# Ternary MLP with Strassen-type layers: the fourth operand difference of each square layer made by VectorE instead of GpSimd

## The reference

```python
Q, K, V = x @ wq.T, x @ wk.T, x @ wv.T                 # D = 64
energy = einsum('bnd,bne->bde', K, V)
x = layernorm(x + ((Q @ energy) * sqrt(3/64)) @ wo.T)
h = silu(x @ w1.T * s1) * (x @ w2.T * s2)              # 256 -> 1024
h = gelu(h @ h1.T * t1)                                # 1024 -> 1024, weights -1, 0, 1 (times 8)
h = gelu(h @ h2.T * t2)                                # 1024 -> 1024
x = layernorm(x + h @ w3.T * s3)                       # 1024 -> 256
```

## Time and profile before

| | us |
|---|---|
| median of 3 runs | 682.74 |
| lowest, highest | 681.18, 683.98 |
| profiled execution | 685.8 |
| its span on the core | 684.0 |
| TensorE matmuls busy | 652.7 (95%) |
| VectorE busy | 473.7 (69%) |
| ScalarE busy | 396.1 (58%) |
| GpSimd busy | 269.5 (39%) |
| mean granted TensorE clock | 0.984 of full speed |

### The profile page before, as it was taken

The page is one execution under the profiler, slowest core; times in us unless marked ns, Lnnn a source line. Parts: engine busy times, 40 slices in busy tenths (PEclk is TensorE's granted clock), DMA queues, the critical chain, the costliest instruction groups (busy, mean ns, idle before and its releaser), DMA issues.

```text
span 684.0 us, 9189 instructions
## 1 busy us (share of the span) xinstructions
PE 652.7 (95%) x3197; PEld 540.7 (79%) x3198; DVE 473.7 (69%) x718; ACT 396.1 (58%) x669; POOL 269.5 (39%) x214
## 2 busy tenths in 40 slices
PE   8978799989999999999999999999999999999992
PEld 7656587878879888688888888688888888888892
DVE  1365457588655898388856799388856799488467
ACT  1366569856764457465854456565755366656660
POOL 1527699169000366049100267039200267077002
PEclk9999999999999999999999999999999999999997
DMA  8997898934440025633440015633340005444101
GB/s 316 410 402 275 301 353 259 333 150 147 146 143 1 0 54 197 242 124 124 129 173 6 1 27 198 252 139 123 124 156 29 1 12 193 165 152 156 63 1 63
DMA packets 24087, 105.02 MB, mean 154 GB/s; under 512 B 2192, under 2 KB 3280, under 8 KB 16208
## 3 DMA queue, kind: packets, MB, share of 16 engines
q1 hardware_dynamic: 24032, 104.29, 43.3%
HBM read 89.60 MB, written 22.02 MB: 163 GB/s over the span
## 4 chain that ended last, share of the span: by engine, by line
PE 78%; DVE 10%; DMA 7%; issue 3%; ACT 1%; SPq 0%; POOL 0%; POOLq 0%; DVEq 0%; ACTq 0%
PE ps L1139 51%; PE ps L1084 16%; PE ps L1196 7%; DVE R L807 4%; DMA xr<-in_xT 2%; DMA w_dram<-in_w2T 2%; DMA w<-w_dram 1%; DVE xr L791 1%; PE ps L1004 1%; PE ps L988 1%; PE ps L1040 1%; DVE quarter L801 1%; DMA out<-xr 1%; PE ps L1026 1%; DVE st L780 1%
## 5 line engine op out<-in xcount | busy, mean ns | idle before, releaser
L1139 PE MATMUL ps<-R,ring 128*128 128x512 f32 x1792 | 414.1, 392 | 4.7 <-issue 4.7
L1139 PEld LDWEIGHTS ps<-R,ring 128*128 128x128 f32 x1792 | 337.7, 189 | 76.6 <-issue 6.6
L807 DVE TENSOR_TENSOR R<-quarter,R 128x512 fp32r<-128x512 f32 x288 | 255.3, 908 | 89.0 <-ACT R L583 88.7
L583 ACT CAST R<-quarter 128x512 fp32r<-128x512 f32 x288 | 175.3, 615 | 26.5 <-POOL quarter L468 10.0
L1084 PE MATMUL ps<-x1T,w 128*128 128x512 f32 x512 | 122.1, 398 | 4.3 <-DVE x1T L751 3.8
L1084 PEld LDWEIGHTS ps<-x1T,w 128*128 128x128 f32 x512 | 97.7, 192 | 26.9 <-issue 2.7
L629 ACT ACTIVATE quarter<-U,sc 128x512 f32<-128x512 f32 x96 | 69.4, 723 | 74.4 <-DVE U L826 32.1
L421 POOL TENSOR_TENSOR ve<-mv,eps 128x4 f32<-128x4 f32 x14 | 5.4, 388 | 235.6 <-DVE mv L784 235.6
L446 POOL TENSOR_TENSOR quarter<-quarter,quarter 128x512 f32<-128x512 f32 x32 | 49.4, 1544 | 118.8 <-ACT quarter L629 109.7
L549 ACT ACTIVATE sg<-ps,sc 128x512 f32<-128x512 f32 x64 | 44.1, 690 | 72.4 <-PE ps L1084 72.2
L599 ACT COPY U<-ps 128x512 f32<-128x512 f32 x96 | 56.3, 586 | 43.1 <-PE ps L1139 43.0
(11 more groups left out here) (66 smaller groups left out, 325.7 us busy)
## 6 DMA issues: line engine op xcount, KB each, us to landing
ring<-combos SPq DMA_DIRECT2D x56, 1024.0 KB, 4.9
combos<-unit SPq DMA_DIRECT2D x8, 1024.0 KB, 8.5
xr<-in_xT SPq DMA_DIRECT2D x13, 512.0 KB, 6.6
unit<-in_h1T SPq DMA_DIRECT2D x4, 1024.0 KB, 11.7
xr<-in_x_rows SPq DMA_DIRECT2D x8, 512.0 KB, 8.0
unit<-in_h2T SPq DMA_DIRECT2D x4, 1024.0 KB, 9.5
out<-xr SPq DMA_DIRECT2D x7, 512.0 KB, 3.0
w<-w_dram SPq DMA_DIRECT2D x3, 1024.0 KB, 8.2
```

The source lines that it names most:

```text
L583: nc.scalar.copy(R[slot_of(p, u)][:, 0, c, :], quarter[operand_home(p, u)][:, c, :]).then_inc(hi_done, 1)
L807: nc.vector.tensor_tensor(r[:, 1, c, :], quarter[operand_home(p, u)][:, c, :], r[:, 0, c, :].bitcast(f32), ALU.subtract).then_inc(lo_done, 1)
L1139: last = nc.tensor.matmul(ps[:, bank + j, :], w, view(R[slot_of(p, u)][:, part, k, :]), start=n in (0, 1, 5) and k == 0 and part == 0, sto ...
```

## The change

The four chunks of the fourth difference, x21 <- x21 - t2, go from GpSimd's `further_differences` to VectorE, into a new function called behind each `lo` of operand u0+2. They get a semaphore of their own, `t4_done`, since two engines can't share one count; `t_done` counts twelve a layer. ScalarE's cast for operand n = 4 and its gelu 1 (which overwrites t2) wait for the new semaphore as well.

```diff
         def n_t(L, i):
-            return 16 * L + i + 1
+            return 12 * L + i + 1
...
-            return {2: 2 * c + 1, 3: 8 + c, 4: 12 + c, 5: 2 * c}[n]
+            return {2: 2 * c + 1, 3: 8 + c, 5: 2 * c}[n]
...
             def further_differences(p, l):
...
-                for c in range(KH):
-                    pool.wait_ge(lo_done, n_split(p, u0 + 1, c))
-                    nc.gpsimd.tensor_tensor(x21[:, c, :], x21[:, c, :], t2[:, c, :], ALU.subtract).then_inc(t_done, 1)
...
-                elif n in (2, 3, 4, 5):
+                elif n == 4:
+                    act.wait_ge(t4_done, KH * L + c + 1)
+                elif n in (2, 3, 5):
                     act.wait_ge(t_done, n_t(L, t_of(n, c)))
...
-                    act.wait_ge(t_done, n_t(L, 15))
+                    act.wait_ge(t_done, n_t(L, 11))
+                    act.wait_ge(t4_done, KH * (L + 1))
...
+            def fourth_difference(p, l, c):
+
+                L, u0 = 2 * p + l, NPROD * l
+                x21, t2 = quarter[homes(p, l)[1]], quarter[homes(p, l)[4]]
+                dve.wait_ge(lo_done, n_split(p, u0 + 1, c))
+                dve.wait_ge(t_done, n_t(L, 2 * c + 1))
+                nc.vector.tensor_tensor(x21[:, c, :], x21[:, c, :], t2[:, c, :], ALU.subtract).then_inc(t4_done, 1)
...
                 for j in range(KH):
                     lo(p, u0 + 2, j)
+                    fourth_difference(p, l, j)
                 for j in range(KH + 1):
                     if j < KH:
                         add_first(L, j)
```

More of the change, by code:

```diff
@@ L176, in build @@
         l1_tile, silu_done, h_made = sem("l1_tile"), sem("silu_done"), sem("h_made")
-        t_done, hi_done, lo_done = sem("t_done"), sem("hi_done"), sem("lo_done")
+        t_done, t4_done, hi_done, lo_done = sem("t_done"), sem("t4_done"), sem("hi_done"), sem("lo_done")
         prod, cp_done, add_done, gelu_done = sem("prod"), sem("cp_done"), sem("add_done"), sem("gelu_done")
@@ L460, in further_differences @@
                 L, u0 = 2 * p + l, NPROD * l
-                x11, x21, _, _, t2 = (quarter[i] for i in homes(p, l)[:5])
+                x11, t2 = quarter[homes(p, l)[0]], quarter[homes(p, l)[4]]
                 for c in range(KH):
```

## The result

The changed kernel took 698.18 us (median of 6 runs, 695.47 to 702.87) against 683.50 for the kernel before (6 runs): ratio 1.0226, 95% interval 1.0181 to 1.027, or 14.7 us more. It is slower, as forecast; the forecast was 20.3 us more, and 698.18 lies inside the range of 694 to 709, in its lower half. Its profiled execution took 697.44 us with a span of 695.7.

What follows compares the result with a forecast made beforehand. TensorE, busy 95% of the span, was taken to bound the kernel; its waits and clock falls over the eight layers summed to 20.3 us, giving 703.0 us on the median of 682.74, range 694 to 709.

Steps and rivals of the forecast that it cites:

- the first rival: Waits of TensorE come but the clock does not fall: 14.7 us more, so 697.4; chance 0.20.
- What bounds, and that the removal gives TensorE nothing directly: TensorE, busy 95% of the span, bounds; ScalarE's casts waited 10.0 us for GpSimd's subtractions, TensorE never did.
- The price of an added instruction: Each added VectorE subtraction: 0.6 us alone, 1.7 beside GpSimd's 128x512 instructions, the high end nearer.
- Layer 2, step by step: First add 6.9 us later, copy done at 268.7, fourth product waits 2.2; layer costs 2.5, layer 4 the same.
- The two delays: Layer 2: the fourth product's wait and the later xr load are the same 2.25 us, not added.
- Layer 0: GpSimd runs without a break; wait of 4.4 us at the fourth product plus 1.7 for the clock: 6.1.
- Layers 6 and 7: Waits of 2.2 and 2.6 us at the fourth products; with the clock 3.9 and 4.3.
- The fall of the clock after them: Half clock after the waits in layers 6 and 7, costing 1.7 us in each.
- Layers 1, 3 and 5: Add 2.5 to 4.8 us later, copy 0 to 1.0 after its turn; cost 0, 0.5 and 0.5.
- The sum: Over layers 0 to 7: 6.1 + 0 + 2.5 + 0.5 + 2.5 + 0.5 + 3.9 + 4.3 = 20.3 us.

Runs made afterwards that it cites:

- late: Changed kernel with the four subtractions still on VectorE but placed behind the layer's first normalisation: 680.35 us, ratio 0.9950 to the kernel before.
- no_third: Changed kernel with GpSimd's L465 (the third difference) left out, output not that of the reference: 680.77 us, ratio 0.9962 to the kernel before.
- the second profile: The changed kernel run once more, nothing altered, for another profile: 699.43 us (4 runs), ratio 1.0198 to the kernel before.

## Why the prediction was right, and where its sizes were off

The range held and the path was right. The central figure, 703.0, is 4.8 us too high, and the first rival (no fall of the clock, 697.4, given 0.20) is nearer to the measured 698.18. Its 14.7 us equals the measured 14.7, but that is a coincidence: it has no fall in layer 0, where there was one, and about 0.5 us each in layers 3 and 5, where there was nothing.

- **What bounds, and that the removal gives TensorE nothing directly.** Right. TensorE is the only engine whose waits count. What GpSimd's relief is worth goes by way of the normalisation (1.38 us instead of 4.30), which here is behind the late adds; `late` shows it, where nothing delays the adds, as the two waits for xr that go.
- **The price of an added instruction.** Right. 0.60 us alone and 1.70 beside GpSimd, four of eight at each price in layer 2. The step rested on reading the low parts of the kernel before in two places with and without GpSimd, and `no_third` shows that GpSimd is the cause.
- **Layer 2, step by step.** The add was forecast 9.3 us after the first low part and came 9.2 after; the copy 6.1 after the add, measured 6.2; TensorE's delay was 2.2, as forecast. The two delays, of the product and of the load for xr, proved to be one: the second wait stayed at 1.10, where it had been 1.39. Layers 2 and 4 took 2.1 and 2.3 us more; the 2.5 had a fall of the clock in it, and the clock stayed at 1.00.
- **Layer 0.** The wait was right: counted from the layer's start, the fourth product starts 4.3 us later than before in the first profile and 4.7 in the second, against 4.4 forecast. (The idle time in brackets, 3.19 and 4.40, differs by more, since in the first profile layer 0 began with 5.2 us at half clock, in the second with 3.4, and TensorE's own lateness eats into the wait.) That the whole came to 6.0 against 6.1 is partly luck: it holds one stretch of 3.4 us at half clock behind the wait, and the second profile had two there, for 7.6 us.
- **Layers 6 and 7.** The waits were right (2.2 and 2.6 forecast; the fourth products start 2.2 us late in both, and the layers are 2.4 us longer). The fall of the clock after them, 1.7 us each, did not come in either profile. This is the term of the sum that was mis-sized: 3.4 us, and 0.5 in layers 2 and 4 with it. I had put gaps of 2.2 us beside the gap of 1.89 with a fall. But 2.2 was the delay of the next matmul's start, and 1.89 an idle time as the profile brackets it; like against like it was 1.6 against 1.89, nearer to the 1.39 without one. Nor was 1.89 the smallest gap with a fall, as the first rival says: the kernel before has a fall at a gap of 1.50 as well, in the front part (TensorE's row, then its clock). The three gaps that I had picked made the clock look more regular than it is.

```profile
43.70 12.74 PE L1084 MATMUL ps<-x1T,w 128*128 128x512 f32 x48 [1.50 <-DVE x1T L751]
```

```profile
43.60:47.10 3.50, 3.40 (x8) 0.51 1.05 417
```

- **Layers 1, 3 and 5.** 0.5 forecast for two of them, 0 measured. The add came 2.4 us late in layer 3, a little less than the 2.5 to 4.8 of the forecast. The eight instructions had only one dear one among them, because L465 came later than I had it, 5.97 us after the first low part instead of 5.42: the two inverse deviations ahead of it (L421, L423) took longer beside VectorE's run. That was just enough. The copy ended at 328.37, and the fourth product was due at 328.94; with one more dear instruction (1.1 us) there would have been a wait of some 0.5, by my estimate from these times.

```profile
315.96 1.77 DVE L816 TENSOR_TENSOR quarter<-quarter,quarter 128x512 f32<-128x512 f32 x1
...
318.26 0.68 DVE L816 TENSOR_TENSOR quarter<-quarter,quarter 128x512 f32<-128x512 f32 x1
```

```profile
320.98 6.18 POOL L465 TENSOR_TENSOR quarter<-quarter,quarter 128x512 f32<-128x512 f32 x4
```

- **The sum.** 20.3 less 3.4 (clock in layers 6 and 7), 0.7 (layers 2 and 4), 1.0 (layers 3 and 5) and 0.2 (layer 0 and the waits of layers 6 and 7) is 15.0. What stays open is the scatter of the changed kernel's runs, 694.95 to 702.87, with mean granted clocks between 0.980 and 0.987: the runs at 702 have the low ones (0.980, 0.981). Against the 0.985 of the profiled execution that is 3 to 3.5 us of lost work, about two stretches at half clock, of the 5 us by which they are longer. Where in the kernel they lay, no trace shows; the second profile has one such stretch more behind the wait in layer 0.

## What to carry to other kernels

Before a piece of work is moved to a less busy engine, look at what stands behind it in that engine's order and how much slack the last reader has: the cost has a threshold there, and below it the move is free. An instruction of VectorE with two SBUF inputs is to be priced by what GpSimd does at that moment, at 0.6 us or 1.7 us for 128x512 float32, not by its mean over the kernel. The same work placed behind the adds, once GpSimd was idle, turned 14.7 us lost into 3 gained.

## What the runs showed of the hardware

VectorE and GpSimd take turns when both run 128x512 float32 instructions with two SBUF inputs: one each in 1.70 us (layer 2 of the changed kernel), where VectorE alone needs 0.60 (`no_third`) and GpSimd alone starts one every 1.36 (near 83 us in the changed kernel). It cuts both ways: tiny instructions of GpSimd are held up by VectorE too. In layer 3 the second pair of L421 and L423 took 0.42 and 1.33 us in the midst of VectorE's subtractions, and 0.20 and 1.01 in the kernel before, where VectorE was reading PSUM. An instruction with one input in PSUM kept its price beside GpSimd (L814, 1.28 us for two).

The clock: the nine profiles of this case have 15 idle times of TensorE of 1.60 to 1.65 us ahead of a fourth product, and after none of them did the granted clock fall from 2.4 to 1.2 GHz. After the idle time of 1.9 us near 141 us (L1048 before the change) it fell in 5 of the nine, after the one of 2.3 us near 61 us in 4 of the nine, and after each of those of 2.17, 2.80, 3.19 (twice) and 4.4 us (twice) ahead of a fourth product. But in the front part, near 43 us, it fell with the idle time of 1.50 us in the kernel before and 1.3 us after the end of one of 1.86 in `late`, and not with those of 1.16 to 1.64 us in the other seven. So the same idle time, in the same kernel, may or may not be followed by a fall, which I had not expected; what decides it stays open. One stretch at half clock moves a run by up to 1.7 us. The 4.40 us of the second profile were followed by two of them. Nor does every stretch cost 1.7 us: where there was none near 144 us, TensorE waited 0.5 to 0.9 us at the next step instead (0.91 for ScalarE in `late`, 0.76, 0.56 and 0.54 in the three others), so that the fall cost about 1 us there.
